# Stack transfers by unit and transposing DMAs by halves in a graph attention kernel

## The reference

```python
h = relu(layernorm(x))
q, k, v = (split_heads(h @ W + b) for each of the three)
scores = q @ k.T / sqrt(32) + beta * adj
scores = where(adj > 0, scores, -9e15)
x = x + softmax(scores) @ v          # heads side by side again
```

## Time and profile before

| | us |
|---|---|
| median of 3 runs | 1089.96 |
| lowest, highest | 1088.49, 1096.8 |
| profiled execution, its own time | 1097.34 |
| profiled execution, span from first to last instruction | 1095.6 |
| mean granted TensorE clock | 0.985 |
| busy PE, DVE, ACT, POOL | 995.5, 934.0, 907.4, 664.4 |
| DMA queue of SP (q1), share of 16 engines' span | 61.7% |

### The profile page before, as it was taken

One profiled execution on the slowest core, in us unless ns is written; L12 is line 12 of the kernel. 1 busy time (PEld: TensorE's weight loads), 2 busy tenths in 40 slices (PEclk: granted clock), 3 DMA queues, 4 the chain that ended last, 5 costly groups with the idle time before them and its releaser, 6 DMA issues.

```text
span 1095.6 us, 33283 instructions
## 1 busy us (share of the span) xinstructions
PE 995.5 (91%) x10587; PEld 673.5 (61%) x10587; DVE 934.0 (85%) x4250; ACT 907.4 (83%) x2378; POOL 664.4 (61%) x908
## 2 busy tenths in 40 slices
PE   4689999999999999999999898999999999999996
PEld 2356666656666666666666566666666666666664
DVE  6469889888898888988899788798888889888898
ACT  3369788878888988888898788888888988888997
POOL 2846656557566666666566656566666656666642
PEclk9899999999999999999999999999999999999999
DMA  4465676647677656667665667656677765667641
GB/s 153 109 145 136 140 170 162 151 117 160 155 177 162 161 143 131 165 160 177 152 161 136 133 163 167 150 148 141 154 161 177 162 140 152 148 154 172 148 118 45
DMA packets 188255, 163.16 MB, mean 149 GB/s; under 512 B 112816, under 2 KB 163504, under 8 KB 188080
## 3 DMA queue, kind: packets, MB, share of 16 engines
q1 hardware_dynamic: 187552, 160.24, 61.7%
q10 hardware_dynamic: 528, 0.79, 0.2%
HBM read 35.91 MB, written 25.17 MB: 56 GB/s over the span
## 4 chain that ended last, share of the span: by engine, by line
PE 40%; issue 10%; SPq 9%; ACT 8%; DMA 4%; DVE 3%; POOL 1%; ACTq 0%; DVEq 0%; POOLq 0%
PE ps_p L442 24%; PE ps_t L462 8%; ACT probs L520 6%; SPq L250 6%; PE ps_s L454 4%; DMA hT<-h_parts 3%; SPq L264 3%; PE ps_o L477 1%; ACT pT L554 1%; DVE biased L644 1%; PE ps_o L478 1%; PE ps_o L479 1%; DVE pT L650 1%; ACT hn L535 1%; POOL on L348 1%
## 5 line engine op out<-in xcount | busy, mean ns | idle before, releaser
L520 ACT ACTIVATE probs<-biased,neg_max 128x128 f32<-128x128 f32 x1536 | 489.8, 392 | 133.5 <-DVE neg_max L644 111.7
L644 DVE CUSTOM_DVE_ANT_0 biased<-ps_s,mask 128x128 f32<-128x128 f32 x1536 | 354.7, 286 | 120.9 <-PE ps_s L454 115.8
L442 PE MATMUL ps_p<-hT,w 128*128 128x512 f16 x1728 | 426.4, 388 | 18.4 <-DMA hT<-h_parts 12.8
L348 POOL TENSOR_TENSOR on<-on,xb 128x384 f32<-128x384 f32 x128 | 127.6, 997 | 284.7 <-DVE on L665 284.7
L442 PEld LDWEIGHTS ps_p<-hT,w 128*128 128x128 f16 x1728 | 170.7, 100 | 179.8 <-issue 32.6
L650 DVE TENSOR_TENSOR pT<-ps_t,pT 128x512 f16<-128x512 f32 x384 | 263.2, 686 | 0.9 <-ACT pT L554 0.2
L462 PE MATMUL ps_t<-ident,probs 128*128 128x128 f32 x1536 | 247.0, 284 | 14.6 <-ACT probs L520 12.1
L554 ACT ACTIVATE pT<-ps_t 128x512 f16<-128x512 f32 x384 | 221.9, 578 | 0.3 <-PE ps_t L462 0.3
L442 PE MATMUL ps_p<-w,hT 128*128 128x384 f16 x1152 | 207.6, 326 | 0.0
L454 PEld LDWEIGHTS ps_s<-k_st,q_st 96*128 96x128 f16 x1536 | 116.1, 98 | 127.8 <-issue 56.1
L454 PE MATMUL ps_s<-k_st,q_st 96*128 96x128 f16 x1536 | 149.8, 219 | 42.5 <-issue 34.9
(11 more groups left out here) (65 smaller groups left out, 998.5 us busy)
## 6 DMA issues: line engine op xcount, KB each, us to landing
q_st<-qT SPq DMA_DIRECT2D x384, 96.0 KB, 2.2
k_st<-kT SPq DMA_DIRECT2D x384, 96.0 KB, 2.2
out<-on SPq DMA_DIRECT2D x128, 192.0 KB, 2.1
xs<-in_x SPq DMA_DIRECT2D x31, 768.0 KB, 5.1
adjs<-in_adj SPq DMA_DIRECT2D x32, 256.0 KB, 5.4
hT<-h_parts SPq DMA_TRANSPOSE x62, 5.7
xs<-in_x ACTq DMA_DIRECT2D x1, 768.0 KB, 7.4
k_st<-in_L_gnn_Wq SPq DMA_DIRECT2D x1, 576.0 KB, 5.2
```

The lines of the kernel that those rows point to most:

```text
L348: pool.tensor_tensor(on[:, j % 2, :], on[:, j % 2, :], xb[:, par, j, :], ALU.add).then_inc(added, 1)
L442: mm = pe.matmul(dst, stationary, moving, start=m == 0, stop=m == MMS - 1)
L520: act.activation(probs[:, odd, i, :], biased[:, odd, i, :], ACT.Exp, bias=neg_max[:, odd, i:i + 1], scale=-1.0).then_inc(exp_done, 1)
L644: dve.tensor_tensor_reduce(out=biased[:, odd, i, :], in0=ps_s[:, i * N:(i + 1) * N], in1=mask[:, gp, v // CH, :], scale=-1.0, scalar=3.0e3 ...
```

## The change

- A spread now takes one unit: `spread(s, par, kind, c)` waits for that unit's low part only and issues three DMAs, one for each block of the stack, of 128 source rows by 512 tokens (128 KB). 18 a step in place of 24 of 96 KB.
- For that the columns of Wq and Wk (and their biases) are reordered when the weights are split at the start: `dims_first` and `heads_first`. Row 4e + i of a unit is dimension e of head place i, and head h of the output is i * 3 + c in place of c * 4 + i. The splitting is done by unit: nine instructions on ACT and nine on DVE in place of three each.
- `h_parts` and `hT` are laid out by graph and then by part. A transposing DMA takes high and low parts of two graphs, and waits for these two alone.
- ACT normalises one graph in each of the slots 3 to 6.
- SP's order in a step is new, as the diff shows. POOL's, PE's and DVE's orders are as before.

```diff
...
         rstd = sb("rstd", [P, G], F32)
         shift = sb("shift", [P, G], F32)
         hn = sb("hn", [P, G, D], F32)
-        h_parts = sb("h_parts", [P, 2, G, D], FP16)
-
-        hT = sb("hT", [P, 2, 2, G, CH, N], FP16)
+        h_parts = sb("h_parts", [P, G, 2, D], FP16)
+
+        hT = sb("hT", [P, 2, G, 2, CH, N], FP16)
         qT = sb("qT", [P, 2, CH, TOK], FP16)
         kT = sb("kT", [P, 2, CH, TOK], FP16)
         q_st = sb("q_st", [P, 2, HPC, CH, TOK], FP16)
...
 
         W_COLS = [slice(n * D, (n + 1) * D) for n in range(3)]
 
+        def heads_first(row):
+            return row.rearrange("p (i e) -> p e i", i=HPC)
+
+        def dims_first(row):
+            return row.rearrange("p (e i) -> p e i", i=HPC)
+
         block = ctx.enter_context(nc.Block())
 
         @block.sync
...
             sp.dma_start(adjs[:], adj_v[0]).then_inc(adj_in, 16)
             sp.dma_start(xs[:, 1], x_v[1]).then_inc(x_in[1], 16)
 
-            def spread(s, par, kind):
+            def spread(s, par, kind, c):
 
                 n, src, dst, landed = (0, qT, q_st, q_in) if kind == "q" else (1, kT, k_st, k_in)
                 wait(sp, scores_done, SLOTS * (s - 1))
                 sp.nop(nofuse=True)
-                wait(sp, qk_low, QK * s + CH * (n + 1))
+                sp.wait_ge(qk_low, QK * s + CH * n + c + 1)
                 sp.nop(nofuse=True)
                 for b, part in enumerate(BLOCKS[kind]):
-                    for i in range(HPC):
-                        sp.dma_start(dst[HD * b:HD * (b + 1), par, i],
-                                     src[HD * i:HD * (i + 1), part]).then_inc(landed, 16)
+                    sp.dma_start(dst[HD * b:HD * (b + 1), par, :, c, :], src[:, part, c, :]).then_inc(landed, 16)
 
             def store(s, j):
 
...
                 sp.nop(nofuse=True)
                 sp.dma_start(out_v[s, j], on[:, j % 2, :]).then_inc(stored[j % 2], 16)
 
-            def turn_tokens(s, par):
+            def turn_tokens(s, par, half):
+                rows = slice(G // 2 * half, G // 2 * (half + 1))
                 wait(sp, proj_done, NB * (s - 1))
-                for a, split in enumerate((h_high, h_low)):
-                    sp.wait_ge(split, G * s)
-                    sp.nop(nofuse=True)
-                    sp.dma_start_transpose(hT[:, par, a].rearrange("p j c t -> p (j c) t"),
-                                           h_parts[:, a].rearrange("p j d -> p (j d)")).then_inc(hT_in, 16)
+                sp.nop(nofuse=True)
+                sp.wait_ge(h_low, G * (s - 1) + G // 2 * (half + 1))
+                sp.nop(nofuse=True)
+                sp.dma_start_transpose(hT[:, par, rows].rearrange("p j a c t -> p (j a c) t"),
+                                       h_parts[:, rows].rearrange("p j a d -> p (j a d)")).then_inc(hT_in, 16)
 
             def step(s, par):
                 proj, attend = 0 <= s <= STEPS - 1, 1 <= s <= STEPS
                 if 2 <= s <= STEPS:
                     store(s - 2, 1)
+                if proj:
+                    spread(s, par, "q", 0)
+                if 2 <= s <= STEPS:
                     store(s - 2, 2)
                 if proj:
-                    spread(s, par, "q")
+                    spread(s, par, "q", 1)
+                    spread(s, par, "q", 2)
                 if 2 <= s <= STEPS:
                     store(s - 2, 3)
+                if 0 <= s <= STEPS - 2:
+                    turn_tokens(s + 1, 1 - par, 0)
+                if proj:
+                    spread(s, par, "k", 0)
+                if 0 <= s <= STEPS - 2:
+                    turn_tokens(s + 1, 1 - par, 1)
+                if proj:
+                    spread(s, par, "k", 1)
                 if 0 <= s <= STEPS - 3:
                     sp.wait_ge(xb_done, G * (s + 1))
                     sp.wait_ge(normed, G * (s + 1))
...
                     sp.wait_ge(mask_done, s + 1)
                     sp.nop(nofuse=True)
                     sp.dma_start(adjs[:], adj_v[s + 1]).then_inc(adj_in, 16)
-                if 0 <= s <= STEPS - 2:
-                    turn_tokens(s + 1, 1 - par)
                 if attend:
                     store(s - 1, 0)
                 if proj:
-                    spread(s, par, "k")
+                    spread(s, par, "k", 2)
                 if s == STEPS:
                     for j in range(1, G):
                         store(s - 1, j)
...
                 pool.wait_ge(normed, G * s + j + 1)
                 wait(pool, hT_in, 32 * (s - 1))
                 pool.nop(nofuse=True)
-                pool.tensor_copy(h_parts[:, 0, j], hn[:, j]).then_inc(h_high, 1)
+                pool.tensor_copy(h_parts[:, j, 0], hn[:, j]).then_inc(h_high, 1)
                 pool.wait_ge(h_high, G * (s - 1) + j + 1)
-                pool.tensor_tensor(h_parts[:, 1, j], hn[:, j], h_parts[:, 0, j], ALU.subtract).then_inc(h_low, 1)
+                pool.tensor_tensor(h_parts[:, j, 1], hn[:, j], h_parts[:, j, 0], ALU.subtract).then_inc(h_low, 1)
 
             def add_bias(s, par, j):
                 wait(pool, x_in[par], 8 * (s - par) + 16)
...
                 if first == 0:
                     bank_free(s, o)
                 if first == 0 and n == 0 and s == 0:
-                    pe.wait_ge(w_low, ("q", "k", "v").index(kind) + 1)
+                    pe.wait_ge(w_low, CH * (("q", "k", "v").index(kind) + 1))
                 for m in range(first, end):
                     c, (a, b) = m // len(PARTS), PARTS[m % len(PARTS)]
                     if o == 0 and s == 0 and m % len(PARTS) == 0:
...
                     if o == 0 and m == 0 and s >= 1:
                         pe.wait_ge(hT_in, 32 * s)
                     if kind == "v":
-                        dst, stationary, moving = bank[:, 0:D], hT[:, par, a, n, c, :], w[:, b, c, 2 * D:3 * D]
+                        dst, stationary, moving = bank[:, 0:D], hT[:, par, n, a, c, :], w[:, b, c, 2 * D:3 * D]
                     else:
                         col = (D if kind == "k" else 0) + n * P
-                        dst, stationary, moving = bank[:], w[:, a, c, col:col + P], hT[:, par, b, :, c, :]
+                        dst, stationary, moving = bank[:], w[:, a, c, col:col + P], hT[:, par, :, b, c, :]
                     mm = pe.matmul(dst, stationary, moving, start=m == 0, stop=m == MMS - 1)
                 if end == MMS:
                     mm.then_inc(proj_done, 1)
...
 
                 j, c = v // CH, v % CH
                 if v == 0:
-                    pe.wait_ge(q_in, 16 * 3 * HPC * (g + 1))
-                    pe.wait_ge(k_in, 16 * 3 * HPC * (g + 1))
+                    pe.wait_ge(q_in, 16 * 3 * CH * (g + 1))
+                    pe.wait_ge(k_in, 16 * 3 * CH * (g + 1))
                 wait(pe, biased_done, HPC * n)
                 for i in range(HPC):
                     mm = pe.matmul(ps_s[:, i * N:(i + 1) * N], q_st[0:STACK, gp, i, c, j * N:(j + 1) * N],
...
                     pe.wait_ge(v_split, G * g + j + 1)
                 pe.wait_ge(p_low_done, n + 1)
                 for i in range(HPC):
-                    h = c * HPC + i
+                    h = i * CH + c
                     o = ps_o[j % 2][:, h * VW:(h + 1) * VW]
                     high, low = pT[:, odd, 0, i, :], pT[:, odd, 1, i, :]
                     first, second = v1[:, gp, j, h, :], v2[:, gp, j, h, :]
...
                     act.activation(v_f[:, n % 2, :], bank[:, 0:D], ACT.Copy).then_inc(v_copied, 1)
                     return
                 if n == 0:
-                    wait(act, q_in if kind == "q" else k_in, 16 * 3 * HPC * s)
+                    wait(act, q_in if kind == "q" else k_in, 16 * 3 * CH * s)
                 dst, b = (qT, 0) if kind == "q" else (kT, 1)
                 act.activation(dst[:, 0, n, :], bank[:], ACT.Identity, bias=bias_qk[:, b, n:n + 1]).then_inc(qk_high, 1)
 
...
                     if proj:
                         for o in ENDED[u]:
                             high_part(s, par, o)
-                    if ahead and u in (3, 4):
-                        for j in range(2 * (u - 3), 2 * (u - 2)):
-                            normalise(s + 1, 1 - par, j)
+                    if ahead and 3 <= u < 3 + G:
+                        normalise(s + 1, 1 - par, u - 3)
 
             for n in range(3):
                 act.wait_ge(w_in[n], 16)
...
 
             def weights_high(n, ready, count):
                 act.wait_ge(ready, count)
-                act.activation(w[:, 0, :, W_COLS[n]], w_raw[:, :, W_COLS[n]], ACT.Copy, scale=SHRINK).then_inc(w_high, 1)
+                for c in range(CH):
+                    out, raw = w[:, 0, c, W_COLS[n]], w_raw[:, c, W_COLS[n]]
+                    if n < 2:
+                        out, raw = dims_first(out), heads_first(raw)
+                    act.activation(out, raw, ACT.Copy, scale=SHRINK).then_inc(w_high, 1)
 
             weights_high(0, wq_scaled, 1)
             for c in range(CH):
...
```

(25 more changed lines are left out.)

## The result

| | before | changed |
|---|---|---|
| median | 1093.38 us (4 runs) | 1215.18 us (4 runs) |
| lowest, highest | 1088.49, 1098.53 | 1209.87, 1219.78 |
| span of the profiled execution | 1095.6 | 1208.1 |
| granted TensorE clock | 0.985 | 0.954 |

The ratio is 1.111, with a 95% interval of 1.103 to 1.119: the change makes the kernel 11% slower. The direction was forecast, the size was not: 1113 with a range up to 1180.

A forecast was written before the change was run, and what follows sets the result against it. The loop through the fourth graph, its split, the residual, SP's queue, x's landing and VectorE's statistics was to close last: 33.68 us a step against 32.69. +28 - 6 + 1 = +23 on 1089.96 gave 1113 us, range 1048 to 1180.

The forecast's parts named there:

- halving gains nothing in a full step: SP: the first half of the transposes stands behind residual 3's store, so it can't go before E + 13.44.
- PE's wait ahead of the scores of slot 3: PE: its wait for k_st at slot 3 (0.41) goes, but the loop does not pass through it.
- E to the fourth graph's end: ScalarE: from starting slot 3's exponentials (E) to the fourth graph normalised, 10.83 us, 4.5 later than before.
- to the residual's end: GpSimd: 0.16 to the split's start, 1.46 from split to residual, 0.99 for the residual; done at E + 13.44.
- SP to the start of x: SP: store 0.63, two transposing halves at 1.74, two groups of three k spreads at 1.90; x starts at E + 21.35.
- x to VectorE's start: Landing of the x load, 5.1 us as in the old trace, giving X = E + 26.45.
- VectorE to the next E: VectorE: statistics and plain queue up to the next slot 3 exponentials, 7.23 us after x lands.
- The end of 0.83: SP: upper end for issuing one spread, 0.63 by 4/3; the forecast took 0.63.
- the sum's own +28: Whole loop: a step of 33.68 against 32.69 us, over the 28 steps from 3 to 30, +28 us.
- The once-only terms: Start of the run: -6 us from the earlier second half in step 0, +1 for splitting weights in nine instructions.
- Rival D: SP: a transpose pays for standing behind any ordinary DMAs, 3.64 each; 37.7 a step, 1225 us; chance 0.13.
- rival B: SP: a transpose issues like an ordinary load or store, 0.52 and a gap; 31.44 a step, 1050 us; chance 0.04.

The follow-up runs named there:

- a3: Changed kernel with the first half of the transposes ahead of the store of residual 3 on SP: 1141.53 us.
- a4: Changed kernel with GpSimd's residual of graph 3 and its bias addition between the splits of graphs 1 and 2: 1049.32 us, 0.967 of before.
- a7: Changed kernel with the second unit's three k spreads behind the loads of x and adj on SP: 1131.72 us.
- a2: Changed kernel with ScalarE normalising two graphs in slot 3 and two in slot 4, as before: 1088.68 us, 1.002 of before.
- b2: Kernel before with only the spreads' part, 18 spreads of one unit each, with reordered weights: 1070.17 us, 0.981 of before.
- a1: Changed kernel with the loads of x and adj right behind the first half of the transposes on SP: 1212.60 us.
- a5: Changed kernel with the diffs of a4 and a1 together: 1044.14 us, 0.957 of before.
- a8: Changed kernel with the diffs of a4, a1 and a2 together: 1061.97 us, 0.973 of before.
- b5: Repeat of b2, the kernel before with only the spreads' part, run for its profile: 1070.88 us.
- b1_single: Kernel before with only ScalarE's part, one graph normalised in each of slots 3 to 6: 1156.99 us, 1.061 of before.

## Why the prediction was right in kind and wrong in size

**Right: what closes the loop.** The members were named in order: fourth graph, splits, residual of graph 3, SP's queue, x, VectorE's statistics. The profile shows each; a3, a4, a7 and a2 each shorten one member, and the time follows. Right too that halving gains nothing in a full step, since the first half stands behind that store; that SP would idle before it (7.0 us); that PE's wait ahead of the scores of slot 3 goes (34.9 us as "issue" before, 0.7 now); and that the shorter packets alone do not make the kernel slower: b2 is faster with them.

**The step that failed: the lengths in the loop's sum.** 33.68 us were forecast, 36.60 measured. No member was missed; all five were sized too small. Forecast beside the turn from 572.84 to 609.71 above, and beside the mean of the 28 turns from step 3 on, read in the same way:

| member | forecast | this turn | how it is read | 28 turns |
|---|---|---|---|---|
| E to the fourth graph's end | 10.83 | 10.92 | 583.06 + 0.70 - 572.84 | 11.02 |
| to the residual's end | 2.61 | 2.97 | 586.73 - 583.76 | 3.00 |
| SP to the start of x | 7.91 | 8.80 | 595.53 - 586.73 | 8.83 |
| x to VectorE's start | 5.10 | 6.69 | 602.22 - 595.53 | 6.03 |
| VectorE to the next E | 7.23 | 7.49 | 609.71 - 602.22 | 7.73 |
| sum | 33.68 | 36.87 | | 36.61 |

Two terms make most of it: SP's way to the start of x, 0.92 us a step too short, of which 0.69 are the six k spreads taken at 0.63 each, and x's landing, taken at 5.10 and 0.93 too short.

- SP. The transposes were the unknown that I feared (1.44 to 3.64 each) and they came out low, 1.48 and 1.43 here; over the run the median is 1.46, the longest 2.95, and with their gaps the two take 1.92 and 1.84 in the mean of the 28 turns where 1.74 was forecast. The spreads cost more than 0.63: to the next instruction's start three took 2.18 and 2.83 us here, 2.27 and 2.22 in the mean, where 1.90 was forecast. The end of 0.83 was in the text, for the range, and I sized by the old DMA's pitch.
- x's landing: 5.9 at the median over the run, 6.7 in this turn. The landing was taken from a place with twelve of the old spreads and a store right ahead of x; here two transposes and six new spreads are. a7 and a3 take three spreads or one transpose away from there and get 5.6 and 5.4; a1, a5 and a8, with one transpose right ahead, 5.5, 5.2 and 5.2; a2 and a4, with the changed kernel's order on SP, 6.3 and 6.4. In b5, where x stands in its old place, it is 4.7 with the new spreads, but there the last of them went out some 4 us before x. So the landing goes with the queue right ahead of x; how much of it is the spreads' new shape was not separated.
- GpSimd. The fourth graph's subtraction takes 1.27 us in place of 0.92. It now falls on slot 7's mask on VectorE (see below), in each of the 28 turns.
- VectorE. 7.23 was the queue without a gap. Here it waits once more, inside slot 2 (0.48 us from one biasing to the next in place of 0.21, at 606.22), where by the profile ScalarE's exponentials of the slot before release it; they had begun late for the same x. Over the run these waits are 5.7 us, 0.2 a step, of the 0.5 that this member is over; some turns have a wait for PE's scores of 1.0 us in it besides.

2.92 us by 28 steps is 82 us, and with the sum's own +28 it gives the 110 that the steps grew by. The once-only terms hardly matter: step 3 begins at 119.62 where it began at 117.98, so the 6 us that I credited to the start did not come.

**What the range did wrong.** Its ends came from single members (a transpose at 3.64, D), while the members that were off, were off together: the spreads' time came from another shape, x's landing from another queue, the subtraction from a moment without that mask. Rival D's time of 1225 was near the result, and its mechanism is not what happened: transposes behind spreads cost 1.46 at the median, and each three spreads held SP for 0.28 and 0.93 us more in the turn above, not 2.4. A good number is not a shown cause.

**The rule of the Trainium skill** (Advanced Engine Details and Errata, X-Bar Transpose (TRN2): transposing DMAs as fast as regular ones) had rival B's 1050 on it. The trace shows 1.43 us of issue where x takes 0.52, so for SP's time, which was what counted, it does not hold here. Whether it holds for the moving of the data no run here separates.

**Where the change's gain went.** a2 against before shows it: spreads by unit are worth 2% alone (b2_units), and by the profile the new SP order uses that up, as it puts x behind both halves and six spreads: from step 3 on a2 waits 22.4 us for x, b5 not at all. The smoother ScalarE is worth 18 us (a8 against a5), and it costs 126 while the residual stands behind the fourth split (after against a2). One order on GpSimd turns the sum from +11% to -3% (a4).

## What to carry to other kernels

Before spreading an engine's work over more slots, look for what is queued in program order behind its last piece, on every engine down the line: here a residual that needed none of it, and behind that a store, two transposes and a load. When a load is moved behind other DMAs, take its landing from a row with such a queue ahead of it, and count that moving one of two late transfers may only change which is late; what helps is releasing both.

## What the runs showed that I had not expected

- Some waits of PE cost more than their length here. After the 3.65 us wait of a1 the granted clock was still 1.00 in the window from 594 to 596, then 0.50 (the level of 1.2 GHz) from 596 to 598, and 0.65 in the next; in the changed kernel a wait of 1.84 us was followed by this:

```profile
597.34 3.09 PE L458 MATMUL ps_p<-hT,w 128*128 128x512 f16 x7 [1.84 <-DMA hT<-h_parts]
```

  Seven matmuls in 3.09 us, 1.67 at full clock. The same group averages 402 ns here, 409 in a1, and 383 in a4. The kernel before's 995.5 us of busy time, scaled by the mean granted clocks (0.985 and 0.954), would be 1028 of the 1034: most of PE's 39 us more at the same work. Not every wait does it: PE's waits in a7 are shorter (in steps 3 to 30, 13 are over 1.5 us, in the changed kernel 41), and its mean clock stays at 0.986.
- A transpose is dearer to issue behind loads than behind spreads: 1.46 us at the median in the changed kernel (but up to 2.95); from step 3 on 3.12 for the half that stands behind x, adj and three spreads in a1. It is the same as the kernel before showed between its first and its second one. In a5 and a8 the half in the same place, mostly 2.6 us behind adj as in a1, took 1.98 and 1.73; what makes the difference no run separates.
- GpSimd's subtraction and VectorE's masks get longer beside each other, and by the trace the one that starts second pays. The third graph's subtraction takes 0.92 us; the fourth's (584.50, shown above) starts 0.24 us behind the mask of slot 7 and takes 1.27:

```profile
581.68 0.92 POOL L344 TENSOR_TENSOR h_parts<-hn,h_parts 128x384 f16<-128x384 f32 x1
```

```profile
584.26 0.74 DVE L631 SCALAR_TENSOR_TENSOR mask<-adjs,beta_col,mask 128x512 f32<-128x512 f32 x1
```

  Four times in b1_single the subtraction started first; it kept its 0.91 or 0.92 us, and the mask took 1.33 to 1.43:

```profile
421.14 0.92 POOL L328 TENSOR_TENSOR h_parts<-hn,h_parts 128x384 f16<-128x384 f32 x1
```

```profile
421.18 1.43 DVE L611 SCALAR_TENSOR_TENSOR mask<-adjs,beta_col,mask 128x512 f32<-128x512 f32 x1
```

  The mask of slot 4 starts behind a subtraction (576.51, 0.92 us) and takes 1.05 us; in the last step, with nothing beside it on GpSimd, it takes 0.42:

```profile
576.65 1.05 DVE L626 TENSOR_SCALAR mask<-adjs 128x512 f32<-128x512 f32 x1
...
1156.70 0.42 DVE L626 TENSOR_SCALAR mask<-adjs 128x512 f32<-128x512 f32 x1
```

  With one graph a slot the subtraction's mean over the run is 1.01 us (the changed kernel) or 1.00 (b1_single), with pairs 0.92. What the two engines share no run tested.
